# A recurrent convolution on one core: W's first piece loaded as 120 + 8 partitions

## What is computed

```python
Wm = W[:, :, 4, 0]                       # 1024 x 1024
def step(carry, x):
    new = relu(einsum('oc,ncw->now', Wm, carry) + b[None, :, None]) + x
    return new, new
xs = moveaxis(group_norm(x), 2, 0)       # 48 rows
_, ys = scan(step, xs[0], xs[1:])        # down
down = concatenate([xs[:1], ys])
_, ys2 = scan(step, down[-1], down[:-1], reverse=True)   # up
return x + moveaxis(concatenate([ys2, down[-1:]]), 0, 2)
```

## Time and profile before

| | us |
|---|---|
| median of 3 runs | 1654.3 (1654.16 to 1655.46) |
| the profiled execution | 1654.27 |
| its span | 1652.5 |
| PE busy in the span | 1547.7 (94%) |
| ACT busy | 1363.4 (83%) |
| DVE busy | 1138.7 (69%) |
| POOL busy | 962.6 (58%) |

### The profile page before, as it was taken

The page is one execution under the profiler, slowest core; times in us unless marked ns, Lnnn a source line. Parts: engine busy times, 40 slices in busy tenths (PEclk is TensorE's granted clock), DMA queues, the critical chain, the costliest instruction groups (busy, mean ns, idle before and its releaser), DMA issues.

```text
span 1652.5 us, 23859 instructions
## 1 busy us (share of the span) xinstructions
PE 1547.7 (94%) x6823; PEld 1279.9 (77%) x6823; DVE 1138.7 (69%) x3337; ACT 1363.4 (83%) x4280; POOL 962.6 (58%) x1107
## 2 busy tenths in 40 slices
PE   0059999999999999999999999999999999999998
PEld 0048888888888888888888888888888888888887
DVE  5786676666766667666676666766667676666766
ACT  5678888888888888888888888888888888888887
POOL 0066676666667666676675555555555555555555
PEclk9999999999999999999999999999999999999999
DMA  9952323232323232231001545444454535353312
GB/s 406 426 223 77 115 77 115 78 115 77 115 81 111 91 102 96 97 103 51 1 1 52 159 130 158 138 149 143 145 160 127 162 125 172 115 172 126 104 53 64
DMA packets 148116, 207.06 MB, mean 125 GB/s; under 512 B 3856, under 2 KB 134928, under 8 KB 145936
## 3 DMA queue, kind: packets, MB, share of 16 engines
q1 hardware_dynamic: 147840, 205.54, 37.1%
q10 hardware_dynamic: 144, 0.00, 0.0%
HBM read 136.32 MB, written 69.21 MB: 124 GB/s over the span
## 4 chain that ended last, share of the span: by engine, by line
PE 93%; DMA 5%; DVE 1%; ACT 0%; issue 0%; SPq 0%; DVEq 0%; ACTq 0%
PE bank L814 31%; PE bank L827 31%; PE bank L821 31%; DMA x_ring<-x_groups 5%; DVE turn L618 1%; PE bank L835 0%; SPq L350 0%; PE bank L873 0%; PE bank L842 0%; PE bank L877 0%; DVE gn_rstd L672 0%; DVE gn_square L665 0%; DVE gn_half L667 0%; DVE turn L652 0%; ACT turn L592 0%
## 5 line engine op out<-in xcount | busy, mean ns | idle before, releaser
L814 PE MATMUL bank<-w_hi,st_hi 128*128 128x512 f32 x2248 | 873.3, 389 | 0.0
L827 PE MATMUL bank<-w_hi,st_lo 128*128 128x512 f32 x2248 | 873.3, 389 | 0.0
L821 PE MATMUL bank<-w_lo,st_hi 128*128 128x512 f32 x2248 | 873.3, 389 | 0.0
L462 POOL TENSOR_TENSOR st_lo<-d_rows,st_hi 128x256 fp32r<-128x256 f32 x650 | 464.4, 739 | 577.3 <-ACT st_hi L579 577.3
L561 ACT ACTIVATE turn<-turn 32x128 f32<-32x128 f32 x2256 | 697.7, 309 | 63.0 <-DVE turn L716 38.9
L722 DVE STREAM_TRANSPOSE turn<-bank 32x128 f32<-32x128 f32 x2256 | 709.4, 314 | 35.5
L827 PEld LDWEIGHTS bank<-w_hi,st_lo 128*128 128x128 f32 x2248 | 421.9, 188 | 87.7
L821 PEld LDWEIGHTS bank<-w_lo,st_hi 128*128 128x128 f32 x2248 | 421.9, 188 | 87.6
L814 PEld LDWEIGHTS bank<-w_hi,st_hi 128*128 128x128 f32 x2248 | 421.9, 188 | 87.5
L572 ACT ACTIVATE turn<-turn,bias_sb 128x128 f32<-128x128 f32 (+1 forms) x1128 | 361.5, 391 | 42.0 <-DVE turn L722 2.4
L579 ACT ACTIVATE st_hi<-d_rows 128x256 fp32r<-128x256 f32 x650 | 237.3, 415 | 138.2 <-DVE d_rows L742 138.1
(11 more groups left out here) (84 smaller groups left out, 169.2 us busy)
## 6 DMA issues: line engine op xcount, KB each, us to landing
x_ring<-x_groups SPq DMA_DIRECT2D x84, 768.0 KB, 8.0
out_groups<-x_ring SPq DMA_DIRECT2D x47, 768.0 KB, 5.1
down_rows<-d_rows SPq DMA_DIRECT2D x40, 768.0 KB, 3.7
d_rows<-down_rows SPq DMA_DIRECT2D x40, 768.0 KB, 6.6
x_ring<-x_groups SPq DMA_DIRECT2D x5, 3072.0 KB, 23.5
d_rows<-x_groups SPq DMA_DIRECT2D x4, 3072.0 KB, 23.8
x_ring<-x_groups SPq DMA_DIRECT2D x4, 1536.0 KB, 10.2
d_rows<-w_halves SPq DMA_DIRECT2D x3, 1024.0 KB, 13.5
```

The lines of the kernel that those rows point to most:

```text
L462: final = pool.tensor_tensor(slot(st_lo, at, b * KB, (b + 1) * KB), d_chunk(row_of(i), i % CHUNKS, b * KB, (b + 1) * KB), slot(st_hi, at, ...
L814: return pe.matmul(bank[j % BANKS][0:used(j), :], stationary(st_hi, j, k), w_cols(w_hi, o, k), start=(n == 0), stop=False)
L821: return pe.matmul(bank[j % BANKS][0:used(j), :], stationary(st_hi, j, k), w_cols(w_lo, o, k), start=False, stop=final)
L827: return pe.matmul(bank[j % BANKS][0:used(j), :], stationary(st_lo, j, k), w_cols(w_hi, o, k), start=False, stop=final)
```

## The change

The first of W's five pieces (tiles 0 to 3, 2048 float32 on each of 128 partitions, 1024 KB) is loaded by two transfers, partitions 0 to 119 and partitions 120 to 127, one behind the other in SP's order and on the same semaphore. ACT's wait for that piece asks for 32 in place of 16. The other four pieces are loaded as before. P is 128.

```diff
 W_PIECES_FRONT = 2
+W_ROWS = (((0, 120), (120, P)),) + (((0, P),),) * (len(W_PIECES) - 1)
@@ load_weights (SP)
-                sp.dma_start(raw_area[:, t0 * HALF:t1 * HALF], w_halves[o, :, n0 * HALF:(n0 + t1 - t0) * HALF]
-                             ).then_inc(w_loaded[n], 16)
+                for p0, p1 in W_ROWS[n]:
+                    sp.dma_start(raw_area[p0:p1, t0 * HALF:t1 * HALF], w_halves[o, p0:p1, n0 * HALF:(n0 + t1 - t0) * HALF]
+                                 ).then_inc(w_loaded[n], 16)
@@ w_round (ACT)
-                act.wait_ge(w_loaded[w_piece(t)], 16)
+                act.wait_ge(w_loaded[w_piece(t)], 16 * len(W_ROWS[w_piece(t)]))
```

## The result

| | before | changed |
|---|---|---|
| median, us | 1654.3 (1653.92 to 1655.48, 11 runs) | 1658.46 (1657.92 to 1659.58, 11 runs) |
| ratio | | 1.0024 (1.0016 to 1.0032) |
| span of the profiled execution | 1652.5 | 1656.3 |

The forecast was 1653.9, with a range up to 1657.1. The measured time is above the range, and the move went the other way than forecast.

A forecast was written before the change was run, and what follows sets the result against it. The prediction took the matmuls to bound the kernel behind 119 us and bytes to pace the head before. From 1654.3, issue 0, wait 0 and -0.44 for the spared laggard gave 1653.9 us, range 1652.9 to 1657.1.

The forecast's parts named there:

- The bound: Behind 119 us only the number of matmuls sets the time; the head, paced by bytes, passes any move to the end.
- Issue and wait: One more issue on SP (0.41 us, covered by 6 us) and ACT's doubled wait for tile 0: each costs 0.
- slack of 2.3 us before tile 0: W's first piece lands at 79.8 and ACT starts on it at 82.08, so only a later landing delays ACT.
- The rate of a row: In W's first load, each engine takes 0.31 us a row, as in today's 2.5 us for 128 rows.
- rival at half rate: The 120 rows run at half rate, 2.5 us more for each engine carrying them: 1655.6 us with laggard spared; chance 0.27.
- The spared laggard: The engine given fewer rows is the lagging one, so the last x piece lands 1.2 us earlier; gain 0.44; chance 0.42.
- The eight rows: The transfer of partitions 120 to 127 adds a ninth row to some engines, priced at 0.31 us.
- Half rate with an unspared laggard: The 120 rows run at half rate and the lagging engine carries them too: 2.5 to 2.8 us later, 1657.1 us.
- The cap of ACT: ACT, busy without a gap from 82.08 to 97.8, can use only 0.44 us of an earlier last x landing.
- Few engines for 120 rows: The 120 rows are dealt to few engines, the fullest setting the pace: up to 35 us, 1689, on one; chance 0.04.
- the one for half rate: Sign: W's first piece lands near 82.3, ACT waits at 82.08 or before 86.26, first matmul comes near 110.
- a sign of being wrong: The prediction is wrong if PE has new gaps behind 119 us or the head changes by over 3 us.

The follow-up runs named there:

- Cols2: Against the kernel before, W's first piece loaded by two transfers cut by columns, each over 128 partitions: 1654.8 us, ratio 1.0000.
- only120: Against the kernel before, only rows 0-119 of W's first piece loaded: 1657.23 us, ratio 1.0017; DVE's step behind both engines' statistics moved by 2.59 us.
- extra8x4: Kernel before plus four unused loads of 8 rows each (every fourth row) behind W's first piece: 1655.37 us, ratio 1.0009; DVE's step behind the statistics moved 1.25 us.
- Extra8: Kernel before plus one unused load of rows 120-127 behind W's first piece: 1655.94 us, ratio 1.0011; DVE's step behind both engines' statistics moved by 2.06 us.
- rows64: Against the kernel before, W's first piece loaded by two transfers, rows 0-63 and rows 64-127: 1658.47 us, ratio 1.0025.

## Why the prediction was wrong

**The bound** held. Only the head mattered, and a move in it arrives at the end nearly whole: +4.07 at the first matmul, +3.8 of span, +4.2 of time. (Rows 3 have 415 to 419 GB/s, and the 430 that the prediction gives with them is in none of the three; nothing hangs on it.)

**Issue and wait** held as mechanisms. Cols2 shows both at nothing. The slack of 2.3 us before tile 0 was read rightly, but it was used up: ACT waits 0.90 us for W.

**The rate of a row** is the step that failed first. The sum took 0.31 us for each of the 120 rows, since the trace had no load of another shape. It stood as a rival at half rate with 2.5 us, at a chance of 0.27; only120 measured +2.59, and the windows have half the bytes a second. The page that the prediction names for it in the Trainium skill (SBUF — State Buffer, "Door 1: The DMA port swizzle") has 196 GB/s for 64 rows and 328 for 128 at 1 MiB; the half that the prediction quotes is its asymptote (218 and 436). What spoke for the rival stood beside it: a full DMA share leaves no room for a loss of rate to hide in. It should have weighed more than the guess that each engine is its own limit. The path differed from that rival's too: the first x piece decided, by way of ACT, and not the last, and the load ahead of W came 1.1 us later, which no case had.

**The spared laggard** is the step that failed second. I took for likeliest that the engine left out is the one that lags. The tail of the changed kernel reads as one engine dry early and another late, and extra8x4 puts the laggard most likely among the eight engines that got a ninth row. By this alone nothing was to be gained. The Trainium skill (DMA: Bandwidth & Descriptors, "Latency and other measured facts") names engines 7 and 15 as the usually slower ones, which left both open, and its best guess at the cause is one of transfers issued from GpSimd, of which the head has none. With its lowest-numbered engines for eight rows, the laggard here would be 7 and not 15. Which number it has no run shows.

**The eight rows** are the term that put the time beyond the range. They stood as one row, 0.31 us. Extra8 measured 2.06. Half rate with an unspared laggard was priced at 2.5 + 0.31 = 2.8, 1657.1; with 2.06 in place of 0.31 it would be 4.6, and the change shows 4.07. I had written that engines would share a way into the memory for the 120 rows and didn't ask the same of eight rows side by side.

**The cap of ACT** held in kind: 0.64 to 0.73 measured, 0.44 forecast, 2.5 by the rival. Reading ACT as without a gap until 97.8 missed 0.15 us of it. It hid what a gain would be worth, and it played no part in a loss.

**Few engines for 120 rows** did not happen (15 reports). Of the signs I named, the one for half rate came true: W's first piece late (ACT waits for it until 84.15), ACT waiting before 86.26's block, the first matmul beyond 110. So did a sign of being wrong: the head changed by over 3 us.

What stays open: why rows 120-127 cost 2.06 us in the full queue and nothing by place when alone. That they hold up the engines behind them on the same partitions fits extra8 and extra8x4, but it is argued, not shown. Nor is it shown why rows64 costs 4.1 and not 2.5, why 112 rows run at 311 GB/s and 120 at 225, or how a row-cut load slows one ahead of it.

## What to carry to other kernels

A DMA share near 1 says that the engines are occupied, not that bytes flow; read the GB/s beside it. Don't cut a load over all 128 partitions into ranges of partitions, however even the halves and however small the rest, while something that the path needs stands behind it or just ahead of it in the queue; a cut by columns was free here. If a range is needed, its place matters: rows 32-95 first cost half of what rows 0-63 and 64-127 did. And price each of the pieces by its own shape: the 64 KB piece cost nearly as much as the 960 KB one.

## What the runs showed of the hardware that I had not expected

Small DVE steps of 0.2 us took 1.1 to 1.3 us each while POOL's subtractions of 1.27 us ran, five of them in the chain that sets the start of the recurrence; without POOL beside them they took 0.2. All five read two operands in SBUF (one of them also writes to PSUM), while the reciprocal at 103.02 and the variance at 102.53, with one operand in SBUF, kept 0.35 and 0.19 although POOL was at work (its two subtractions from 102.14 on). The Trainium skill (SBUF — State Buffer, "Who interferes with whom") states that a DVE instruction with two SBUF inputs and a GpSimd instruction that reads SBUF exclude each other; the trace agrees, and it was worth 4.2 us, as much as the change that was studied, and in the other direction.
